# Expert stage of a perceiver layer: biases as matmuls, one Relu a tile, rows normalised by ScalarE, GpSimd only scatters

## The reference, cut to what matters

```python
x = x + xattn(layernorm(x), ctx_768, ...)      # 4096 tokens (128 sequences of 32), 128 channels
x = x + rwkv_attn(layernorm(x), ...)
xf = layernorm(x).reshape(4096, 128)
expert_idx = argmax(xf @ Wr.T + br, axis=-1)   # one of 8 experts for each token
h = relu(einsum('td,efd->etf', xf, W1) + b1[:, None, :])   # 512 hidden channels
y = einsum('etf,edf->etd', h, W2) + b2[:, None, :]
out = x + y[expert_idx, arange(4096)]
```

## Time and profile before

| | |
|---|---|
| median of 3 runs | 1026.3 us (1025.68 to 1027.58) |
| span of the profiled execution | 1027.0 us |
| PE busy | 870.6 us (85%) |
| DVE busy | 831.1 us (81%) |
| POOL busy | 774.3 us (75%) |
| ACT busy | 684.0 us (67%) |
| drain of the mix and tables | about 800 to 826 us |
| routing, then scatter to `sorted_rows` | 828 to 863, 863.65 to 907.9 us |
| 40 expert tiles | 909.84 to 1020.8 us |

### The profile page before, as it was taken

The page is one execution under the profiler, slowest core; times in us unless marked ns, Lnnn a source line. Parts: engine busy times, 40 slices in busy tenths (PEclk is TensorE's granted clock), DMA queues, the critical chain, the costliest instruction groups (busy, mean ns, idle before and its releaser), DMA issues.

```text
span 1027.0 us, 29818 instructions
## 1 busy us (share of the span) xinstructions
PE 870.6 (85%) x8554; PEld 720.6 (70%) x8554; DVE 831.1 (81%) x2343; ACT 684.0 (67%) x2029; POOL 774.3 (75%) x1237
## 2 busy tenths in 40 slices
PE   7989998999999999999999999999998461049895
PEld 7777786878787887878787887887776261036664
DVE  5899888989999989899999999998988657025563
ACT  3777776778777778778777777777775113037774
POOL 5788888898989898888889898989886503735554
PEclk9999999999999999999999999999999655559998
DMA  9111111111111111111111211111100840111120
GB/s 233 33 33 33 32 33 33 33 33 36 49 42 32 31 31 31 31 31 31 31 31 32 59 33 31 31 31 31 31 2 2 129 162 14 52 43 53 47 54 17
DMA packets 56836, 45.11 MB, mean 44 GB/s; under 512 B 8367, under 2 KB 54578, under 8 KB 56769
## 3 DMA queue, kind: packets, MB, share of 16 engines
q1 hardware_dynamic: 54464, 40.01, 15.9%
q0 software_dynamic: 2304, 4.25, 1.3%
HBM read 37.25 MB, written 7.52 MB: 44 GB/s over the span
## 4 chain that ended last, share of the span: by engine, by line
PE 36%; POOL 31%; issue 13%; DVE 12%; ACT 4%; DMA 1%; POOLq 1%; DVEq 1%; ACTq 0%; SPq 0%
POOL Pn L925 10%; PE bank L396 6%; PE bank L373 6%; PE bank L420 4%; POOL cT L916 4%; PE bank L1369 3%; PE bank L413 3%; PE bank L385 3%; POOL sorted_rows L1232 3%; POOL chi L906 2%; PE bank L1384 2%; DVE cs L839 2%; DVE nmax L783 2%; POOL clo L910 2%; DVE Tl L777 1%
## 5 line engine op out<-in xcount | busy, mean ns | idle before, releaser
L925 POOL TENSOR_TENSOR Pn<-Pe,rsum 128x1028 f32<-128x1028 f32 x128 | 243.1, 1899 | 74.4 <-DVE rsum L798 74.4
L713 ACT ACTIVATE Pe<-bank,nmax 128x257 f32<-128x257 f32 x512 | 240.5, 475 | 30.1 <-DVE nmax L783 29.5
L783 DVE TENSOR_REDUCE nmax<-bank 128x1 f32<-128x257 f32 x512 | 202.0, 415 | 35.3 <-PE bank L373 34.0
L373 PE MATMUL bank<-cT,qh 96*128 96x257 f16 x1024 | 184.8, 275 | 21.1 <-ACT Pe L713 19.6
L777 DVE TENSOR_TENSOR Tl<-bank,Th 128x512 f16<-128x512 f32 x256 | 173.8, 680 | 0.5 <-ACT Th L702 0.4
L702 ACT ACTIVATE Th<-bank 128x512 f16<-128x512 f32 x256 | 141.3, 595 | 48.5 <-PE bank L420 48.5
L420 PE MATMUL bank<-identf,Pn 128*128 128x128 f32 x1024 | 149.3, 274 | 0.0
L373 PE MATMUL bank<-cT,ql 96*128 96x257 f16 x512 | 139.2, 272 | 0.0
L420 PEld LDWEIGHTS bank<-identf,Pn 128*128 128x128 f32 x1024 | 115.1, 142 | 6.1
L373 PEld LDWEIGHTS bank<-cT,qh 96*128 96x128 f16 x1024 | 90.3, 97 | 38.3 <-issue 15.9
L713 ACT ACTIVATION_READ_ACCUMULATOR Pe<-bank,nmax 128x1 f32 x512 | 103.8, 203 | 0.0
(11 more groups left out here) (213 smaller groups left out, 2444.4 us busy)
## 6 DMA issues: line engine op xcount, KB each, us to landing
rawT<-in_dram SPq DMA_DIRECT2D x32, 385.5 KB, 3.9
raw<-in_dram SPq DMA_DIRECT2D x32, 384.0 KB, 4.4
sorted_rows<-fill SPq DMA_DIRECT2D x1, 2620.0 KB, 21.1
xs<-sorted_rows SPq DMA_DIRECT2D x40, 65.5 KB, 1.8
R<-in_dram SPq DMA_DIRECT2D x4, 512.0 KB, 5.9
Z<-last_rows SPq DMA_DIRECT2D x128, 2.2 KB
w1r<-in_dram SPq DMA_DIRECT2D x4, 512.0 KB, 13.7
w2fr<-in_dram SPq DMA_DIRECT2D x4, 512.0 KB, 14.2
```

Of the source, the lines that this page charges most:

```text
L373: last = nc.tensor.matmul(bank[SB[t]][:, 0:M], w[:, par, b, t * P:(t + 1) * P], cT[:, s4, c, 0:M], start=(k == 0), stop=(k == 2))
L713: nc.scalar.activation(Pe[:, n_par(j + 1), t, :], bank[SB[t]][:, 0:M], ACT.Exp, bias=nmax[:, n_par(j + 1), t:t + 1], accum_out=sums[:, n_p ...
L783: nc.vector.tensor_reduce(nmax[:, n_par(j + 1), t:t + 1], bank[SB[t]][:, 0:M], AX.X, ALU.max, negate=True).then_inc(s_nmax, 1)
L925: nc.gpsimd.tensor_tensor(Pn[:, par, :, :], Pe[:, par, :, :], rsum[:, par, :].unsqueeze(2).broadcast_to([P, QT, M]), ALU.mult)\
```

## The change

The bias of each product becomes one more matmul at the head of its group. `bias` holds for each expert the four rows of b1 and the row of b2 as float16 on partitions 0 to 4, and the rest of each value on partitions 32 to 36; `pick` is a 0/1 matrix that selects the rows. ACT's four Relus and its copy become one Relu from PSUM to `hh`; DVE takes `hl` straight from PSUM as max(x, 0) - hh. The normalising step `xsn` moves from DVE to ACT, with -mean/std as bias and 1/std as scale, in front of the Relu. The row number is stored as an integer and read by the scatter from `xs` directly, so `yb`, `idx` and POOL's add go; `xs` has 12 buffers. POOL waits no longer for `s_te` before its first scatter. New work in the setup: POOL clears `biasf` (128 x 1024 float32) as its first step after the last cross attention result, and builds `pick` and `bias` after its last mixing step.

```diff
@@ SP, setup @@
-            sp.dma_start(b1T[:, :], b1T_d).then_inc(s_small, 16)
+            sp.wait_ge(s_bias, 1)
+            for r0 in (0, LO):
+                sp.dma_start(biasf[r0:r0 + FC + 1, :, :], bias_d).then_inc(s_small, 16)
             sp.dma_start(brb[:, :], br...broadcast_to([P, E])).then_inc(s_w3, 16)
-            sp.dma_start(b2b[:, :, 0:C], b2...broadcast_to([P, E, C])).then_inc(s_w3, 16)
@@ SP, tiles @@
-                wait(sp, s_t["xn"], s - UN + 1)
-                wait(sp, s_t["yb"], s - UN + 1)
+            for s in range(NT):
+                if s >= XB:
+                    sp.wait_ge(s_store[(s - XB) % UN], 16 * ((s - XB) // UN + 1))
+                sp.dma_start(xs[:, s % XB, :], sorted_rows[P * s:P * (s + 1), :]).then_inc(s_xs[s % XB], 16)
@@ POOL @@
             pool.wait_ge(s_res, GB * G)
+            nc.gpsimd.memset(biasf[:, :, :], 0.0).then_inc(s_bias, 1)
...
-            nc.gpsimd.memset(b2b[:, :, C:C + 1], 0.0).then_inc(s_ftab, 1)
...
             drain_mix(pool_step)
+            for a, part in enumerate((pick, pick2)):
+                nc.gpsimd.memset(part[:, :, :], 1.0).then_inc(s_pick, 1)
+            pool.wait_ge(s_pick, 2)
+            for a, part in enumerate((pick, pick2)):
+                nc.gpsimd.affine_select(out=part[:, :, :], in_=part[:, :, :], compare_op=ALU.is_equal, fill=0.0,
+                                        base=-LO * a, pattern=[[-1, FC + 1], [0, P]], channel_multiplier=1)\
+                    .then_inc(s_pick, 1)
+            pool.wait_ge(s_pick, 4)
+            nc.gpsimd.tensor_tensor(pick[:, :, :], pick[:, :, :], pick2[:, :, :], ALU.add).then_inc(s_pick, 1)
+            pool.wait_ge(s_small, 48)
+            nc.gpsimd.tensor_copy(bias[:, :, :], biasf[:, :, :]).then_inc(s_bias, 1)
             pool.wait_ge(s_fill, 16)
             pool.wait_ge(s_row, 2)
             pool.wait_ge(s_pos, 1)
-            pool.wait_ge(s_te, 1)
...
-                    nc.gpsimd.tensor_tensor(yb[:, w, :], xs[:, w, 0:C + 1], b2b[:, bass.ds(e, 1), :]..., ALU.add)
+            for s in range(NT):
+                pool.wait_ge(s_t["out"], s + 1)
+                nc.gpsimd.indirect_dma_start(out_rows, IndirectOffsetOnAxis(ap=xs[:, s % XB, C:C + 1].bitcast(U32), axis=0),
+                                             yout[:, s % UN, :], ...).then_inc(s_store[s % UN], 16)
@@ ACT @@
-                    for f in range(FC):
-                        last = nc.scalar.activation(hr[:, v, f, :], bank[2 + v][:, f * P:(f + 1) * P], ACT.Relu,
-                                                    bias=b1T[:, bass.ds(FC * e + f, 1)])
...
-                    nc.scalar.activation(hh[:, u % UN, :, :], hr[:, u % 2, :, :], ACT.Copy)
+            for s in range(-3, NT):
+                if s + 3 < NT:
+                    k = s + 3
+                    act.wait_ge(s_xs[k % XB], 16 * (k // XB + 1))
+                    wait(act, s_t["xT"], k - 1)
+                    nc.scalar.activation(xsn[:, k % 2, :], xs[:, k % XB, 0:C], ACT.Identity,
+                                         scale=xs[:, k % XB, C + 2:C + 3], bias=xs[:, k % XB, C + 1:C + 2])
+                if s >= 0:
+                    wait(act, s_t["y"], s - 3)
+                    wait(act, s_t["h"], s + 1)
+                    nc.scalar.activation(hh[:, s % UN, :, :], bank[2 + s % 2][:, :]..., ACT.Relu)
+                if 0 <= s + 2 < NT:
+                    (xsh of s + 2, as before)
@@ PE, tile s @@
                     wait(pe, s_t["xl"], s + 1)
-                    wait(pe, s_t["hr"], s - 1)
+                    wait(pe, s_t["hl"], s - 1)
                     pe.wait_ge(s_w3l, 2 * E)
+                    pe.wait_ge(s_bias, 3)
+                    pe.wait_ge(s_pick, 5)
+                    nc.tensor.matmul(bank[2 + v][:, :], bias[:, bass.ds(e, 1), :]...,
+                                     pick[:, 0:FC, :]..., start=True, stop=False)      # 512 columns
...
                     wait(pe, s_t["hl"], s - 1)
                     wait(pe, s_t["out"], s - 3)
-                    pe.wait_ge(s_w3l, 2 * E)
+                    nc.tensor.matmul(bank[4 + v][:, 0:C], pick[:, FC, :],
+                                     bias[:, bass.ds(e, 1), :]..., start=True, stop=False)      # 128 columns
@@ DVE @@
+            nc.vector.tensor_tensor(bias[LO:LO + FC + 1, :, :], biasf[...], bias[...], ALU.subtract)   # behind W1l, W2l
+            for s in range(-2, NT + 2):
+                if 0 <= s < NT:
+                    wait(dve, s_t["y"], s - 3)
+                    wait(dve, s_t["hh"], s + 1)
+                    nc.vector.scalar_tensor_tensor(hl[:, s % UN, :, :], bank[2 + s % 2][:, :]..., 0.0,
+                                                   hh[:, s % UN, :, :], ALU.max, ALU.subtract)
+                if 0 <= s + 2 < NT:
+                    (xsl of s + 2, as before)
+                if 0 <= s - 2 < NT:
+                    (yout of s - 2: bank + xs, waits for y of s - 2)
```

More of the change, by code:

```diff
@@ L300, in perceiver_layer_kernel @@
         brb = lsb("brb", [P, E])
-        b1T = lsb("b1T", [P, E * FC])
-        b2b = lsb("b2b", [P, E, C + 1])
+        biasf = lsb("biasf", [P, E, P])
+        bias = lsb("bias", [P, E, P], F16)
+        pick = lsb("pick", [P, FC + 1, P], F16)
+        pick2 = lsb("pick2", [P, FC + 1, P], F16)
         desc = lsb("desc", [P, E])
@@ L1053, in expert @@
                 return experts[s]
-            for it in range(NT // UN + 2):
-                for u in range(1 - UN, 1):
-                    step(it, u, lambda v: expert(UN * it + v))
+            return expert
         def dve_var(chain):
@@ L1233, in _ @@
                                              R[:, g, :], None, bounds_check=NT * P - 1).then_inc(s_sorted, 16)
[L1235 to L1253, removed]
+            for s in range(NT):
+                pool.wait_ge(s_t["out"], s + 1)
+                nc.gpsimd.indirect_dma_start(out_rows,
+                                             bass.IndirectOffsetOnAxis(ap=xs[:, s % XB, C:C + 1].bitcast(U32), axis=0),
+                                             yout[:, s % UN, :], None, bounds_check=TOK - 1, oob_is_err=False)\
+                    .then_inc(s_store[s % UN], 16)
         @block.scalar
@@ L1304, in _ @@
-            over_tiles(act, act_tile)
+            for s in range(-3, NT):
[4 more added lines that the diff above has]
+                    nc.scalar.activation(xsn[:, k % 2, :], xs[:, k % XB, 0:C], ACT.Identity,
+                                         scale=xs[:, k % XB, C + 2:C + 3],
+                                         bias=xs[:, k % XB, C + 1:C + 2]).then_inc(s_t["xn"], 1)
+                if s >= 0:
+                    wait(act, s_t["y"], s - 3)
+                    wait(act, s_t["h"], s + 1)
+                    nc.scalar.activation(hh[:, s % UN, :, :], bank[2 + s % 2][:, :].rearrange("p (f t) -> p f t", f=FC),
+                                         ACT.Relu).then_inc(s_t["hh"], 1)
+                if 0 <= s + 2 < NT:
+                    k = s + 2
+                    wait(act, s_t["h"], k - 1)
+                    wait(act, s_t["xT"], k + 1)
+                    nc.scalar.activation(xsh[:, k % 2, :], bank[k % 2][:, 0:P], ACT.Copy).then_inc(s_t["xh"], 1)
@@ L1356, in _, with pe_tile @@
             pe.wait_ge(s_te, 1)
[L1359 to L1363, removed]
+            def pe_tile(s, expert):
+                v = s % 2
+                if 0 <= s < NT:
+                    e = expert(s)
                     wait(pe, s_t["xl"], s + 1)
-                    wait(pe, s_t["hr"], s - 1)
+                    wait(pe, s_t["hl"], s - 1)
                     pe.wait_ge(s_w3l, 2 * E)
+                    pe.wait_ge(s_bias, 3)
+                    pe.wait_ge(s_pick, 5)
+                    nc.tensor.matmul(bank[2 + v][:, :], bias[:, bass.ds(e, 1), :].rearrange("p o c -> p (o c)"),
+                                     pick[:, 0:FC, :].rearrange("p f t -> p (f t)"), start=True, stop=False)
                     for f in range(FC):
@@ L1490, in dve_tile @@
+            nc.vector.tensor_tensor(bias[LO:LO + FC + 1, :, :], biasf[LO:LO + FC + 1, :, :], bias[LO:LO + FC + 1, :, :],
+                                    ALU.subtract).then_inc(s_bias, 1)
+            for s in range(-2, NT + 2):
+                if 0 <= s < NT:
                     wait(dve, s_t["y"], s - 3)
                     wait(dve, s_t["hh"], s + 1)
-                    nc.vector.tensor_tensor(hl[:, u % UN, :, :], hr[:, u % 2, :, :], hh[:, u % UN, :, :], ALU.subtract)\
-                        .then_inc(s_t["hl"], 1)
@@ new lines, in _ @@
+                if 0 <= s + 2 < NT:
+                    k = s + 2
+                    wait(dve, s_t["h"], k - 1)
+                    wait(dve, s_t["xh"], k + 1)
+                    nc.vector.tensor_tensor(xsl[:, k % 2, :], bank[k % 2][:, 0:P], xsh[:, k % 2, :], ALU.subtract)\
+                        .then_inc(s_t["xl"], 1)
+                if 0 <= s - 2 < NT:
+                    k = s - 2
+                    if k >= UN:
```

(3 more changed lines are left out.)

108 lines of the change are left out of this document (31 added, 77 removed).

## The result

The changed kernel is slower: 1036.29 us median (1036.27 to 1041.43, 4 runs) beside 1026.94 (1025.68 to 1028.81, 4 runs) of before, ratio 1.0111 with a 95% interval of [1.0093, 1.0129] (the two medians alone give 1.0091). The sign was forecast, the size was not: 1029.5 was named, with 1034.5 as the upper end.

The account below looks back on a forecast made before the run. The prediction took PE's instruction issue to bound the tiles. Tiles +5.5, memset +0.8, pick steps +0.1, scatters -1.4, start -0.5 and end -1.3 gave +3.2: span 1030.2, median 1029.5 us, range 1024.3 to 1034.5.

Parts of the forecast that it names:

- The pair of matmuls: PE, each tile: two bias matmuls with an address of their own add 0.06 + 0.06 us each, 0.24.
- The waits: PE, each tile: two waits added before the W1 group, one gone before the W2 group, 0.05 us each.
- The relief: Tiles 4 to 39: with less work on ACT and DVE, PE's waits for `xsn` go, -4.6 us.
- The pick and bias steps beside DVE: Setup, in POOL's idle time before the first scatter: may slow DVE's normalising a little, +0.1 us (0 to 0.5).
- The scatters: First scatter waits for `pos` instead of `pk`, starting 2.45 us earlier: -1.4 us (0 to -2.4).
- The start of the tiles: First W1 group can start some 1.6 us earlier with `xsn` on ACT; taken as -0.5 (-1.5 to +0.5).
- The base: Sum made against the profiled span of 1027.0 us, with the median of the runs 0.7 below it.
- x: What PE gets more to issue each tile, matmul pair and waits: 0.29 us, bounds 0.11 to 0.45.
- no change to be told: Rival: x of about 0.15 to 0.25, or a start gaining its full 1.5; 1026 to 1028 us; same: 0.24.
- array on top: Rival: the 512-column matmul's array time isn't made up; x 0.45, tiles +11.1, 1035.1 us; chance 0.18.
- The queue hides the pairs: Rival: PE's queue runs ahead, x falls to 0.11, tiles -0.8, 1023.2 us; chance 0.15.
- tables: Rival: Identity and Relu need different ACT tables, two loads a tile, 1040 us or far above; chance 0.01.

Follow-up runs that it names:

- before again: The kernel before, with nothing changed, profiled once more; span 1024.1 us, tiles 4 to 39 in 87.82 us.
- experiment 3: Changed kernel with PE's three waits on constants (low weights, biases, `pick`) once ahead of the tiles; 1033.57 us, ratio 1.0056.
- experiment 4: Changed kernel without its bias matmuls, the two added waits (`s_bias`, `s_pick`) moved ahead of the tiles; 1025.56 us, ratio 0.9971 to before.
- experiments 7 and 10: Kernel before with the wait for `s_te` moved behind the 32 scatters, then the same profiled again; tiles 4 to 39 took 86.62 us both times.
- Experiment 7: Kernel before with one line moved, the wait for `s_te` behind the 32 scatters; 1028.27 us, ratio 1.0002.
- experiment 1: Changed kernel without its bias matmuls, b1 and b2 left out, its waits kept; 1030.19 us, ratio 1.0017 to before.
- experiment 2: Changed kernel with the first bias matmul over 128 columns instead of 512; ratio 1.0121 to before.
- experiments 8 and 11: Changed kernel, constant waits and `pk` loads ahead of tiles, setup steps moved; 8: b2 by GpSimd's add, ratio 0.9951; 11: both bias matmuls kept, ratio 1.0000.

## Why the prediction was right or wrong

Right was the bound: a tile is as long as PE's issue, so whatever goes from ACT and DVE to PE is paid in full. The sum was +3.2, and the spans differ by 10.2 against before again (7.3 against the profile that the forecast used). The median lies 1.8 above the top of the range. Term by term:

- **The pair of matmuls**, 2 x 0.12 a tile, 8.4: measured 8.8. Right. That the 512 columns vanish in the 0.07 that each block leaves free was right too.
- **The waits**, a net of one at 0.05 a tile, 1.75: measured 4.4. This is the first mis-sized term. The 0.05 was read from a single place, the wait pair ahead of the transpose, as 0.13 less 0.06. I counted semaphores, and what the runs show as paid for are instructions. In the W1 group three waits became five, by the trace 2 + 1 (one `EVENT_SEMAPHORE` and the register step) and 2 + 2 + 1 (two and the register step): one more instruction, 0.125 a tile, and the gap of 0.27 in before is 0.39 in after. In the W2 group three became two, 2 + 1 (L1381: 202, 236; register step L1384: 233) and 1 + 1 (one `EVENT_SEMAPHORE`: 244; register step L1371: 242), so the instructions are as many, and from the transpose to the first matmul of the group 0.21 us pass in both (982.97 to 983.18 in before, 982.95 to 983.16 in after): nothing came back for the wait that went. To take out `s_w3l` as well (experiment 3, 4.3) brought no more than the two alone (experiment 4, 4.4): either way one instruction goes.
- **The relief**, -4.6: the mechanism was right and PE never waits for `xsn` again. Against the profile used it is 4.1, against before again 2.1, against the two calm profiles of experiments 7 and 10 only 0.9. The term was read from one execution that had more of these waits than the next. This is the second mis-sized term.
- **The memset**, +0.8: +0.9. Right.
- **The pick and bias steps beside DVE**, +0.1 (0 to 0.5): +2.1. The third term, and outside its own bounds. I asked only whether POOL was idle, 39 us of it, and not what DVE did in that time; "slow DVE a little" had no row behind it. A step of 0.2 us stood for 1.44 beside one on GpSimd.
- **The scatters**, -1.4: -1.6, and the scatter behind `pos` started where it was put (1.22 behind it). Experiment 7 gives 1.3 of it to the wait alone.
- **The start of the tiles**, -0.5: -1.1. The first W1 group starts 2.24 behind the first `xsn` instead of 3.37. No run shows the 1.1 us that the forecast held against its gain of 1.6. What the runs show in its place is the pair of bias matmuls: without it (experiment 1) the stage is 10.51, 0.9 less, and only 0.26 of that is columns (experiment 2). The clock moved this stage little: in experiment 7 the granted clock is already 1.00 in the slice 917 to 918, in before it is 0.66 as late as 921 to 922, and both need the same 12.5 us for this stage.
- **The end**, -1.3: -1.3, last scatter at 6.25 for the 6.3 worked out. Right.
- **The base.** The median was put 0.7 under the profiled run. It is nearer to 2, since a run's time is about 2 more than its span. In the total this and the relief are largely one error seen from two sides: of the 2.9 us that the profiled execution was longer than before again, 2.0 lie in the tiles, where it waited more for `xsn`, and 1.0 ahead of the tables. The base moves by more than that from round to round, 1026.94 to 1030.42.

One sum of the forecast is off by itself: x of 0.15 gives 3.2 - 35 x 0.14 = -1.7, so the rival *no change to be told* reaches down to 1024.6 and not to 1026.

The misses add up: waits 2.6, relief 2.5, pick steps 2.0, pair 0.4, cross attention 0.2 and memset 0.1, less 0.6 for the start and 0.2 for the scatters, make 7.0, the difference between 10.2 and 3.2.

Of the rivals, *array on top* would have given 1035.1, nearest to the 1036.3 measured, and is false: experiment 2 takes the columns away and nothing moves, and the weight load behind the bias matmul of the tile above starts at 981.96, beside that matmul (981.84, 0.39 long) and 0.10 ahead of its own. Its number is near the result by luck; the spacing of W1, (98.84 - 4 x 0.67) / 35 = 2.75, fell between the marks that I had set (2.6 to 2.7, and 2.8), and only an experiment could tell. *The queue hides the pairs* is refuted by experiment 1, *tables* by ACT's 38.75 busy us in 98.84 and by the trace of after, whose last `ACT_TABLE_LOAD` lies at 817.7 (817.5 in before, whose tiles alternate Relu and Copy). The cover for the new wait on `hl` holds: `hl` is there 2.4 us or more ahead.

## What to carry to other kernels

Where an engine's issue is the bound, its instruction stream is the budget: count every wait instruction and address step in the inner loop, look in the trace at how many instructions the waits became, take waits on constants out of the loop (4.3 us here, without touching the work), and leave to idle engines what they do beside it, even if a matmul could do it (4.2 us here). Before steps are put into GpSimd's idle time, read what DVE does in just that time (2.1 us here). And a term that is a sum of small stalls should be read from two executions of the profile, or be given the width that lies between them.

## What the runs showed of the hardware that was not expected

- Waits that were long met cost time in PE's queue, by the instruction: one `EVENT_SEMAPHORE` less at the head of the W1 group took 4.4 us off 35 tiles where two waits went with it (experiment 4) and 4.3 where three did (experiment 3), 0.12 a tile, as much as the second bias matmul with its address step (4.2 us, experiments 8 and 11). In PE's tiles one such instruction has one or two semaphores in the trace (L1366 of before: 202 and 231), and the register step behind it one more (L1369: 229). The profile puts that time down to whoever signalled last (`hl`, 21 times, 3.9 us; 0.2 once the constant waits are out).
- At a granted clock of 1.00 the bias matmul cost as much with 512 columns as with 128, among matmuls whose issue is the bound (98.84 and 98.83 us in 35 tiles), though the one behind it starts 0.22 later. In the stage ahead, in part at 0.50, it was 11.39 and 11.13.
- Some DVE steps stood still to the end of a GpSimd step: 0.21 us became 1.44, four norms of 1.10 became 3.98. Others did not: the two `BATCH_NORM_STATS2` beside POOL's steps for `pick` took 0.49 together (826.54), as in before. GpSimd's scatters suffered the other way round: beside DVE's subtractions of the weights they followed each other 1.80 us apart (1.49 and 0.30 in the rows above) and 1.28 otherwise.
- A GpSimd memset of 1024 float32 took 0.95 us.
- Kernels with the same code in the tiles differed by 3.2 us there (86.62 to 89.84), in stalls of some 0.3 us at `xsn`. What sets them off stays open.
